# Graph kernel, first layer's dense turns: chunks taken alternately from a unit's halves, chunk tables streamed a turn at a time, a deeper ring of moving one-hots

## The chip, the cores and the metric

The kernel runs on one core of a Trainium2 chip. The metric is the device time of one execution in microseconds, as the median of several executions. TensorE appears as PE (weight loads as PEld), VectorE as DVE, ScalarE as ACT, GpSimd as POOL, SyncE as SP.

## The reference

6,250 nodes with 256 features, 200,000 edges sorted by destination, each with a weight. The part that this case is about is the first of two graph convolutions:

```
def _graph_conv(x, W, edge_src, edge_dst, edge_weight, n_nodes):
    support = x @ W
    msg = support[edge_src] * edge_weight[:, None]
    return jax.ops.segment_sum(msg, edge_dst, num_segments=n_nodes)
...
h = _graph_conv(features, W1, edge_src, edge_dst, edge_weight, n)
out = _graph_conv(h, W2, edge_src, edge_dst, edge_weight, n)
...
x = x + gnn(xn) + mix(xn)            # xn = layernorm(x); mix: linear attention
x = x + moe(layernorm(x))            # 16 experts, 2 a row
```

Both segment sums are done on unweighted features (the products with W1 and W2 are joined and come later), so that a layer is: for each destination node, the weighted sum of the rows of its sources.

## The kernel before

The edges lie in 1,584 chunks of 128. Each layer takes them in two ways at once. 768 chunks are **gathered**: GpSimd fetches the 128 source rows of a chunk by an indirect DMA (`gathers`, L606), and PE multiplies them with one-hots of the destination (`gathered`, L924). Four chunks make a step, 192 steps a layer, six steps a unit of 128 destinations. The other 810 chunks are **dense**: 27 units (turns) of 30 chunks. A dense turn has two stages.

*Build.* For each chunk PE multiplies a one-hot of the source's low 7 bits, times the weight (`lo_hot`, DVE, L1280, 128x128), with a moving one-hot of the pair of source tile and destination (`moving`, ACT, two activations L707 and L709, 128x343), into one of three PSUM banks (`build_chunk`, L899). DVE adds the 128x343 result into the slab, a 128 x 49 x 128 matrix in SBUF, at a destination offset that a register holds (`add_chunk`, L1295). Neighbouring chunks write overlapping columns, as the destinations are sorted, so an add waits for the add before it (`s_bev`). Rings: 10 `lohot`, 10 `mvs`, 3 banks; PE's chunk c waits for the add of chunk c-3.

*Apply.* When the last add is done, SP stores the slab's seven planes to DRAM (L477; the second layer loads them again), and PE multiplies the 49 slab tiles with the node features (`apply`, L911, seven tiles a plane). ACT clears each plane (`blanks`, L714) once it is applied and stored; the first add of the next turn waits for all seven (`s_z`). Meanwhile the first 10 `lo_hot` and `moving` of the next turn are made, two a plane.

The dense and gathered sums go through `take_dense` or `takes` (ACT copies, L732, L725), a placement matmul on PE (`place_dense` L943, `place_gathered` L934; their one-hots are `dense_hots` and `gathered_hots`, L1324) and an add by DVE into the layer's result (`place_add`, L1335). A turn also holds seven or eight gathered steps, at chunks 4, 11, 18, 25 and after planes 0, 2, 4 (and 5) (`SLOT1`), and DVE's destination one-hots for them (`half_hots`, L1317, L1319).

Every order is written out by hand; each engine runs its own list, held together by counting semaphores. The per-chunk numbers (`lo`, `nkey`, `off`) are computed once at the start by DVE and stay in SBUF (`l1tab`). In the second layer the slabs are only loaded and applied, then come the mix, the experts and the output.

## Time and profile before

| | |
|---|---|
| time, median of 3 | 3638.55 us (3625.0 to 3643.43) |
| the profiled execution | 3613.85 us, of which the profile's span is 3612.2 us |
| first layer's dense turns | from 78.4 us to about 1515 us of the span |
| PE busy over the span | 2916.3 us (81%) |
| DVE, ACT, POOL busy | 39%, 40%, 51% |
| mean granted TensorE clock | 0.927 of full speed |

The engines' busy shares are means over stages with different limits. In a line of the timeline stand the start and the length of a group of instructions, the engine, the line of the kernel, what it writes and reads, the count, and in brackets how long the engine was idle before and what it waited for.

### The profile page before, as it was taken

What the parts mean: (1) busy time and instruction counts of PE and PEld (TensorE: products, weight loads), DVE (VectorE), ACT (ScalarE), POOL (GpSimd) and SP (SyncE); (2) the same over time, 40 slices, a digit from 0 to 9 for tenths busy, and PEclk for the clock granted to TensorE, in tenths of its full rate; (3) what the DMA queues carried; (4) which work ended last, traced back from release to release, by engine and by line L of the source; (5) the groups of instructions that cost most, each with busy time, mean ns of one, the idle gap of its engine ahead of it and who ended that gap; (6) DMA issues with size and microseconds to landing.
All of it is one profiled execution on the core that took longest, in us unless ns stands there. A gap on an engine that the chain in (4) does not pass through costs nothing.

```text
span 3612.2 us, 49615 instructions
## 1 busy us (share of the span) xinstructions
PE 2916.3 (81%) x14732; PEld 2068.0 (57%) x14733; DVE 1420.1 (39%) x3945; ACT 1455.2 (40%) x3127; POOL 1844.7 (51%) x1924
## 2 busy tenths in 40 slices
PE   1799999899989999768988888888877648988930
PEld 0466556556656665546655666566546647777830
DVE  7544554554455446322222222222215541111157
ACT  4677776777777777300000000000004423333322
POOL 3555555545555555256666666666643651222235
PEclk9899999999999999979998999999988869999975
DMA  6344434434443443375555555555532334444454
GB/s 217 119 137 142 143 108 142 142 103 143 146 139 114 141 146 131 104 236 173 177 173 167 174 178 177 164 178 176 174 93 88 119 123 131 135 142 131 118 155 125
DMA packets 257759, 525.92 MB, mean 146 GB/s; under 512 B 47793, under 2 KB 144056, under 8 KB 257337
## 3 DMA queue, kind: packets, MB, share of 16 engines
q1 hardware_dynamic: 142492, 263.69, 22.4%
q0 software_dynamic: 84240, 228.40, 21.0%
q10 hardware_dynamic: 30832, 31.42, 2.7%
q8 instruction: 99, 1.62, 0.2%
q14 instruction: 96, 0.79, 0.1%
HBM read 387.33 MB, written 137.44 MB: 145 GB/s over the span
## 4 chain that ended last, share of the span: by engine, by line
PE 52%; issue 12%; DVE 11%; another core or an unknown queue 10%; ACT 6%; DMA 5%; SPq 3%; DVEq 1%; ACTq 1%; POOL 0%; POOLq 0%
PE bank L911 28%; PE bank L899 8%; PE sums L924 5%; DVE pa L1295 4%; DMA pa<-ys_d 4%; PE bank L1134 3%; PE bank L988 2%; PE bank L934 1%; ACT build L709 1%; ACT build L707 1%; PE sums L882 1%; ACT pa L833 1%; PE bank L943 1%; SPq L537 1%
## 5 line engine op out<-in xcount | busy, mean ns | idle before, releaser
L606 POOL DMA_INDIRECT pa<-xn_d,srcs x768 | 739.8, 963 | 667.4 <-PE sums L924 481.6
L606 POOL DMA_INDIRECT pa<-h_d,srcs x768 | 756.1, 985 | 398.2 <-issue 212.6
L911 PE MATMUL bank<-t1s,pa 128*128 128x256 f32 x2646 | 657.6, 398 | 100.0 <-issue 79.8
L899 PE MATMUL bank<-build 128*128 128x343 f32 x1620 | 559.9, 477 | 130.5 <-DVE build L1280 54.7
L1295 DVE TENSOR_TENSOR pa<-bank,pa 128x343 f32 x810 | 417.4, 515 | 603.8 <-ACT pa L714 462.8
L911 PE MATMUL bank<-t0s,pa 128*128 128x256 f32 x2646 | 612.5, 389 | 45.2 <-DVE pa L1295 37.4
L911 PEld LDWEIGHTS bank<-t1s,pa 128*128 128x128 f32 x2646 | 515.8, 199 | 231.5 <-issue 143.2
L911 PEld LDWEIGHTS bank<-t0s,pa 128*128 128x128 f32 x2646 | 504.7, 194 | 155.4 <-issue 86.2
L899 PEld LDWEIGHTS bank<-build 128*128 128x128 f32 x1620 | 279.8, 192 | 376.1 <-issue 298.1
L709 ACT ACTIVATE build<-build,ones 128x343 f32<-128x343 f32 x810 | 471.3, 582 | 26.3
L707 ACT ACTIVATE build<-build,l1tab 128x343 f32<-128x343 f32 x810 | 458.8, 566 | 37.3 <-issue 24.6
L665 POOL DMA_INDIRECT eo_d<-pa,eplc x109 | 107.3, 984 | 389.5 <-DVE pa L1614 348.2
L924 PE MATMUL sums<-pa,hots 128*32 128x256 f32 x3072 | 279.0, 399 | 33.5 <-issue 31.1
L714 ACT ACTIVATE pa<-zero 128x896 f32<-128x896 f32 x182 | 172.3, 947 | 330.2 <-PE bank L911 274.8
L1421 DVE TENSOR_REDUCE l1tab<-build 128x8 f32<-128x512 f32 x49 | 33.6, 686 | 592.6 <-ACT build L759 367.8
L1280 DVE TENSOR_SCALAR build<-iota_n,l1tab,wts 128x128 f32<-128x128 f32 x810 | 263.7, 353 | 0.0
L754 ACT ACTIVATE build<-bank 128x256 f32<-128x256 f32 x49 | 18.8, 384 | 502.0 <-remote 408.8
L1134 PE MATMUL bank<-build,pa 128*128 128x128 f32 x1744 | 218.0, 279 | 0.2 <-ACT build L845 0.2
L1134 PEld LDWEIGHTS bank<-build,pa 128*128 128x128 f32 x1744 | 208.1, 196 | 0.7 <-issue 0.6
L1122 PE MATMUL bank<-pa 128*128 128x256 f32 x872 | 207.6, 381 | 0.0
L1614 DVE TENSOR_TENSOR pa<-bank,pa 128x256 f32<-128x256 f32 x109 | 46.3, 425 | 389.2 <-PE bank L1122 389.2
L924 PEld LDWEIGHTS sums<-pa,hots 128*32 128x32 f32 x3072 | 69.1, 109 | 200.9 <-issue 199.4
(247 smaller groups left out, 2565.9 us busy)
## 6 DMA issues: line engine op xcount, KB each, us to landing
slab_d<-pa SPq DMA_DIRECT2D x189, 448.0 KB
pa<-slab_d SPq DMA_DIRECT2D x189, 448.0 KB
pa<-in_w ACTq DMA_DIRECT2D x32, 512.0 KB, 4.0
pa<-in_w SPq DMA_DIRECT2D x32, 512.0 KB, 3.7
pa<-ys_d SPq DMA_DIRECT2D x109, 130.0 KB
pa<-eo_d SPq DMA_DIRECT2D x49, 256.0 KB, 3.2
pa<-xn_d,srcs POOLq DMA_INDIRECT x768
pa<-h_d,srcs POOLq DMA_INDIRECT x768
```

The source lines that it names most:

```text
L606: pool.indirect_dma_start(gath[g % RING * QT + j], None, table, bass.IndirectOffsetOnAxis(ap=srcs[:, n:n + 1], axis=0)).then_inc(s_g[g % R ...
L665: pool.indirect_dma_start(eo_d, bass.IndirectOffsetOnAxis(ap=eplc[b][:], axis=0), eo[b], None, bounds_check=NONE - 1, oob_is_err=False).th ...
L707: act.activation(a, iotaw, ACT.Abs, bias=nkey[:, c:c + 1]).then_inc(s_mt, 1)
L709: act.activation(a, a, ACT.Relu, bias=ones[:, 0:1], scale=-1.0).then_inc(s_mv, 1)
L714: act.activation(plane(p), zero[:].broadcast_to([P, CT * P]), ACT.Copy).then_inc(s_z, 1)
L899: pe.matmul(bld[c % BLD][:, 0:WT], lohot[c % LR], mvs[c % MR], start=True, stop=True).then_inc(s_bmm, 1)
L911: ins = pe.matmul(app[:, 0:D], slab3[:, s, :], table[:, s * D:(s + 1) * D], start=s == 0, stop=s == T - 1)
L924: ins = pe.matmul(bank[u % 2][j * Q:(j + 1) * Q, 0:D], hoth[g // HK % HB][:, k % HK, j, :], gath[g % RING * QT + j], start=k == 0, stop=k ...
L1122: ins = pe.matmul(bank[4 + b][:, 0:D], hT[b][:, f, :], we2[b][:, f, :], start=f == 0, stop=f == 3)
L1134: ins = pe.matmul(bank[2 + b][:, f * P:(f + 1) * P], we1[b][:, a, f * P:(f + 1) * P], eyT[b][:, a, :], start=a == 0, stop=a == 1)
L1280: dve.tensor_scalar(lohot[c % LR], iota_n[:], lo[:, c:c + 1], wts[:, C0 + c:C0 + c + 1], ALU.is_equal, ALU.mult).then_inc(s_lo, 1)
L1295: dve.tensor_tensor(part, bld[c % BLD][:, 0:WT].rearrange("p (s w) -> p s w", w=W), part, ALU.add).then_inc(s_bev, 1)
```

## The change

Each unit's 30 chunks are now taken as 0, 15, 1, 16, ... (`chunk_at`), so that two adds in a row never touch the same columns of the slab, and an add waits only for the add before the last (except in the last turn). A flag at the start tests that such chunks lie at least seven destinations apart. The ring of moving one-hots grows from 10 to 18, of which 15 (three a plane) are made during the apply before; `lohot` from 10 to 12. SBUF for it comes from the tables: these go to DRAM at the start (`tab_d`, `off_d`), and SP loads 30 columns of them for each turn, two turns ahead, before it stores the slab. The dense unit's `place_add` and `dense_hots` move from the build (chunks 6 and 20) to the apply (planes 0 and 3).

```diff
-LR = 10
-MR = 10
+LR = 12
+MR = 18
+EARLY_LO = 12
+EARLY_MV = 15
+TABS = 2
...
-CREDIT = 12
+CREDIT = 20
 AHEAD = 4
-EARLY = 2
...
+        tab_d = dram("tab_d", [P, 2 * DC])
+        off_d = dram("off_d", [1, DC], I32)
...
-        l1tab = sb("l1tab", [P, 3 * DC])
+        tabs = [sb(f"tabs{b}", [P, 3, KB]) for b in range(TABS)]
+        offs = [sb(f"offs{b}", [1, KB], I32) for b in range(TABS)]
...
+        def chunk_at(m):
+
+            return m // 2 + m % 2 * (KB // 2)
...
+            sp.wait_ge(s_tab, 1)
+            sp.dma_start(tab_d, tab).then_inc(s_tst, 16)
+            sp.dma_start(off_d, off[0:1, :]).then_inc(s_tst, 16)
+            sp.wait_ge(s_tst, 32)
+
+            def turn_tables(i):
+                b = i % TABS
+                sp.wait_ge(s_lo, (i - TABS) * KB + KB)
+                sp.wait_ge(s_mv, (i - TABS) * KB + KB)
+                c = i * KB
+                sp.dma_start(tabs[b][:, 0:2, :], tab_d.rearrange("p (k c) -> p k c", k=2)[:, :, c:c + KB]).then_inc(s_tl[b], 16)
+                sp.dma_start(tabs[b][:, 2, :], wt_t[:, C0 + c:C0 + c + KB]).then_inc(s_tl[b], 16)
+                sp.dma_start(offs[b][:], off_d[:, c:c + KB]).then_inc(s_tl[b], 16)
+
             for i in range(NU):
                 sp.wait_ge(s_bev, i * KB + KB + BLD)
+                if i + TABS < NU:
+                    turn_tables(i + TABS)
                 for p in range(CT):
                     sp.dma_start(rows(slab_d, i)[:, p * CT * P:(p + 1) * CT * P], plane(p)).then_inc(s_slab[p], 16)
...
-            pool.memset(t1s[:, NCH + DC:T * D], 0.0).then_inc(s_t1z, 1)
+            pool.memset(t1s[:, SCRATCH:T * D], 0.0).then_inc(s_t1z, 1)
             pool.wait_ge(s_tab, 1)
-            pool.memset(t1s[:, 0:NCH + DC], 0.0).then_inc(s_t1z, 1)
+            pool.wait_ge(s_tst, 32)
+            pool.memset(t1s[:, 0:SCRATCH], 0.0).then_inc(s_t1z, 1)
             pool.wait_ge(s_xst, 16 * NC)
...
-            def moving(c):
-
+            def moving(i, m):
+
+                c = i * KB + m
                 a = mvs[c % MR]
+                if m == 0 and i >= TABS:
+                    act.wait_ge(s_tl[i % TABS], 48 * (i // TABS))
                 act.wait_ge(s_bmm, c - MR + 1 + CREDIT)
-                act.activation(a, iotaw, ACT.Abs, bias=nkey[:, c:c + 1]).then_inc(s_mt, 1)
+                k = chunk_at(m)
+                act.activation(a, iotaw, ACT.Abs, bias=tabs[i % TABS][:, 1, k:k + 1]).then_inc(s_mt, 1)
                 act.wait_ge(s_mt, c + 1)
                 act.activation(a, a, ACT.Relu, bias=ones[:, 0:1], scale=-1.0).then_inc(s_mv, 1)
...
-            for c in range(MR):
-                moving(c)
+            for m in range(EARLY_MV):
+                moving(0, m)
             for i in range(NU):
                 for m in range(KB):
-                    if m + MR < KB:
-                        moving(i * KB + m + MR)
+                    if m + EARLY_MV < KB:
+                        moving(i, m + EARLY_MV)
                     takes(steps_at(i, "m", m, 0), 0)
                 for p in range(CT):
                     if i < NU - 1:
-                        for m in range(p * EARLY, min(MR, (p + 1) * EARLY)):
-                            moving(i * KB + KB + m)
+                        for m in range(p * 3, min(EARLY_MV, (p + 1) * 3)):
+                            moving(i + 1, m)
                         blanks(i, p)
...
+            apart = exc.rearrange("p (k c) -> p k c", c=KB)[:, 0:NU - 1, 0:KB // 2 + 1]
+            off3 = off.rearrange("p (k c) -> p k c", c=KB)[:, 0:NU - 1, :]
+            link(dve.tensor_tensor(apart, off3[:, :, KB // 2 - 1:KB], off3[:, :, 0:KB // 2 + 1], ALU.subtract))
+            link(dve.tensor_reduce(reg[:, 4:5], apart, AX.XY, ALU.min))
+            link(dve.tensor_scalar(reg[:, 4:5], reg[:, 4:5], float(W), None, ALU.is_ge))
             link(dve.tensor_scalar(reg[:, 0:1], reg[:, 0:1], float(Q - 1), None, ALU.is_le))
+            link(dve.tensor_tensor(reg[:, 0:1], reg[:, 0:1], reg[:, 4:5], ALU.mult))
...
+            late_half = off.rearrange("p (k c) -> p k c", c=KB)[:, :, KB // 2:KB]
+            link(dve.tensor_scalar(reg[:, 5:6], reg[:, 3:4], float(P // 2), None, ALU.mult))
+            link(dve.tensor_scalar(off, off, reg[:, 1:2], None, ALU.mult))
+            link(dve.tensor_scalar(late_half, late_half, reg[:, 5:6], None, ALU.add))
...
+            for b in range(TABS):
+                link(dve.tensor_copy(tabs[b][:, 0:2, :], tab.rearrange("p (k c) -> p k c", k=2)[:, :, b * KB:(b + 1) * KB]))
+                link(dve.tensor_copy(offs[b][:], off[0:1, b * KB:(b + 1) * KB]))
...
-            def lo_hot(c):
-
+            def lo_hot(i, m):
+
+                c, k, a = i * KB + m, chunk_at(m), tabs[i % TABS]
                 dve.wait_ge(s_bmm, c - LR + 1 + CREDIT)
-                dve.tensor_scalar(lohot[c % LR], iota_n[:], lo[:, c:c + 1], wts[:, C0 + c:C0 + c + 1],
-                                  ALU.is_equal, ALU.mult).then_inc(s_lo, 1)
-
-            def offsets(c):
+                dve.tensor_scalar(lohot[c % LR], iota_n[:], a[:, 0, k:k + 1], a[:, 2, k:k + 1], ALU.is_equal, ALU.mult
+                                  ).then_inc(s_lo, 1)
+
+            def offsets(i):
+                if i >= TABS:
+                    dve.wait_ge(s_tl[i % TABS], 48 * (i // TABS))
                 return nc.values_load_multi_w_load_instructions(
-                    off[0:1, c:c + KB], engines=[mybir.EngineType.DVE], min_val=0, max_val=P - W,
+                    offs[i % TABS][0:1, :], engines=[mybir.EngineType.DVE], min_val=0, max_val=P - W,
                     skip_runtime_bounds_check_because="it is bounded by the subtraction from the span's end")[1]
 
-            def add_chunk(c, at):
-
-                if c % KB == 0:
-                    dve.wait_ge(s_z, c // KB * CT + CT)
+            def add_chunk(i, m, at):
+
+                c = i * KB + m
+                if m == 0:
+                    dve.wait_ge(s_z, i * CT + CT)
                 dve.wait_ge(s_bmm, c + 1 + CREDIT)
-                dve.wait_ge(s_bev, c + BLD)
-                part = slab3[:, :, bass.ds(at, W)]
+                dve.wait_ge(s_bev, c + BLD - (0 if i == NU - 1 else 1))
+                part = slab3[:, :, bass.ds(at[chunk_at(m)], W)]
...
-            for c in range(LR):
-                lo_hot(c)
+            for m in range(EARLY_LO):
+                lo_hot(0, m)
             dve.wait_ge(s_t1z, 2)
+            at = offsets(0)
             for i in range(NU):
-                at = offsets(i * KB)
                 for m in range(KB):
-                    c = i * KB + m
-                    add_chunk(c, at[m])
-                    if m + LR < KB:
-                        lo_hot(c + LR)
-                    if m == 6 and i > 0:
+                    add_chunk(i, m, at)
+                    if m + EARLY_LO < KB:
+                        lo_hot(i, m + EARLY_LO)
+                    all_gathered(steps_at(i, "m", m, 0), 0, t1s)
+                if i < NU - 1:
+                    at = None
+                    at = offsets(i + 1)
+                for p in range(CT):
+                    if p == 0 and i > 0:
                         place_add(1, GU + i - 1, t1s)
-                    if m == 20:
-                        dense_hots(i, 0)
-                    all_gathered(steps_at(i, "m", m, 0), 0, t1s)
-                for p in range(CT):
                     all_gathered(steps_at(i, "p", p, 0), 0, t1s)
                     if i < NU - 1:
-                        for m in range(p * EARLY, min(LR, (p + 1) * EARLY)):
-                            lo_hot(i * KB + KB + m)
+                        for m in range(p * 2, min(EARLY_LO, (p + 1) * 2)):
+                            lo_hot(i + 1, m)
+                    if p == 3:
+                        dense_hots(i, 0)
```

Not shown are moved scratch regions: the tables are computed in `t1s`, and the second layer's small weights, which lay in `l1tab`, now lie in `build`.

Three places in the instruction lists. First DVE, from the last add of a turn to the first add of the next one, before (L1295 is the slab add, L1280 `lo_hot`, L1317 and L1319 `half_hots`; TENSOR_LOAD fetches the 30 offsets):

```order
L1295 TENSOR_TENSOR pa<-bank,pa 128x49x7
L1317 TENSOR_TENSOR hots<-iota_n,drel 128x384
L1319 TENSOR_TENSOR hots<-hots,wts 128x384
L1280 TENSOR_SCALAR build<-iota_n,l1tab,wts 128x128 x10
L1284 TENSOR_LOAD l1tab
L1295 ISA
```

and after (L1349 is the slab add, L1331 `lo_hot`, L1371 and L1373 `half_hots`, L1389 `place_add`, L1378 `dense_hots`):

```order
L1349 TENSOR_TENSOR pa<-bank,pa 128x49x7
L1337 TENSOR_LOAD offs
L394 TENSOR_LOAD t_i
L394 ISA x2
L1389 ISA
L1389 TENSOR_TENSOR t1s<-bank,t1s 128x512
L1371 TENSOR_TENSOR hots<-iota_n,drel 128x384
L1373 TENSOR_TENSOR hots<-hots,wts 128x384
L1331 TENSOR_SCALAR build<-iota_n,tabs 128x128 x8
L1378 TENSOR_SCALAR hotp<-iota_n,drow 128x128 x2
L1331 TENSOR_SCALAR build<-iota_n,tabs 128x128 x4
```

The loads, the placement's add and its one-hots now stand in the apply stage, and 12 instead of 10 `lo_hot` do.

Second ACT, between the clearing of two planes in the apply stage, before (L714 clears a plane):

```order
L714 ACTIVATE pa<-zero 128x896
L707 ACTIVATE build<-build,l1tab 128x343
L709 ACTIVATE build<-build,ones 128x343
L707 ACTIVATE build<-build,l1tab 128x343
L709 ACTIVATE build<-build,ones 128x343
L714 ACTIVATE pa<-zero 128x896
```

and after (L751 clears a plane, L744 and L746 make a moving one-hot):

```order
L751 ACTIVATE pa<-zero 128x896
L744 ACTIVATE build<-build,tabs 128x343
L746 ACTIVATE build<-build,ones 128x343
L744 ACTIVATE build<-build,tabs 128x343
L746 ACTIVATE build<-build,ones 128x343
L744 ACTIVATE build<-build,tabs 128x343
L746 ACTIVATE build<-build,ones 128x343
L751 ACTIVATE pa<-zero 128x896
```

Three moving one-hots stand between two planes up to the fifth, where two stood.

Third SP's queue after the change, from the start's last stores through the first turn's slab stores; before, the slab stores (L477) followed directly on the stores of `xn_d`:

```order
L488 DMA xn_d<-t0s 128x7x256 x7
L491 DMA tab_d<-t1s 128x1620
L492 DMA off_d<-t1s 1x810
L500 DMA tabs<-tab_d 128x2x30
L501 DMA tabs<-in_wt_t 128x30
L502 DMA offs<-off_d 1x30
L509 DMA slab_d<-pa 128x896 x7
```

Two stores are new at the start, and three small loads stand ahead of the seven slab stores of each of the first 25 turns.

## Rows read from the trace of the kernel before

**Rows 1.** Busy time by stretch, one dense turn a row; first the first turn

```profile
core 0: us, PE busy (x) PEld busy (x) DVE busy (x) ACT busy (x) POOL busy (x), PEclk, DMA share, GB/s
78.42:150.91 72.49, 54.59 (x216) 32.66 (x216) 25.94 (x70) 44.58 (x80) 44.05 (x46) 0.81 0.41 130
...
412.18:463.22 51.04, 47.24 (x224) 31.11 (x223) 26.48 (x71) 38.58 (x70) 27.14 (x28) 1.00 0.41 136
...
515.39:573.92 58.53, 51.01 (x233) 32.62 (x231) 28.61 (x78) 38.58 (x70) 29.56 (x31) 0.94 0.37 122
...
1412.50:1462.42 49.92, 47.39 (x224) 31.04 (x223) 27.05 (x73) 38.59 (x70) 27.22 (x28) 1.00 0.42 139
```

**Rows 2.** Groups by line, 150 to 1500 us: PE's two large ones

```profile
L911 PE MATMUL bank<-t0s,pa 128*128 128x256 f32 x2500 | 579.4, 389 | 43.9 <-DVE pa L1295 36.2 <-issue 7.8
L899 PE MATMUL bank<-build 128*128 128x343 f32 x1560 | 530.5, 471 | 59.7 <-DVE pa L1295 35.4 <-issue 12.4 <-ACT build L709 11.8
```

**Rows 3.** Timeline of DVE in the build of the turn at 412.18

```profile
428.31 0.56 DVE L1317 TENSOR_TENSOR hots<-iota_n,drel 128x384 f32<-128x384 f32 x1
...
429.81 0.69 DVE L1335 TENSOR_TENSOR t1s<-bank,t1s 128x512 f32 x1 [0.35 <-issue]
430.42 0.50 DVE L1295 TENSOR_TENSOR pa<-bank,pa 128x343 f32 x1
430.84 0.34 DVE L1280 TENSOR_SCALAR build<-iota_n,l1tab,wts 128x128 f32<-128x128 f32 x1
431.12 0.52 DVE L1295 TENSOR_TENSOR pa<-bank,pa 128x343 f32 x1
...
437.04 0.52 DVE L1295 TENSOR_TENSOR pa<-bank,pa 128x343 f32 x1 [0.20 <-DVE pa L1295]
437.76 0.52 DVE L1295 TENSOR_TENSOR pa<-bank,pa 128x343 f32 x1 [0.20 <-issue]
```

**Rows 4.** Timeline of PE in the same turn: build's end, apply, next build

```profile
431.07 3.06 PE L899 MATMUL bank<-build 128*128 128x343 f32 x8 [1.82 <-DVE pa L1295]
...
434.63 2.58 PE L899 MATMUL bank<-build 128*128 128x343 f32 x8
438.42 3.26 PE L911 MATMUL bank<-t0s,pa 128*128 128x256 f32 x14 [1.21 <-DVE pa L1295]
441.61 0.64 PE L924 MATMUL sums<-pa,hots 128*32 128x256 f32 x8
...
461.95 1.90 PE L899 MATMUL bank<-build 128*128 128x343 f32 x6
```

**Rows 5.** Timeline of ACT in two apply stages

```profile
441.78 0.95 ACT L714 ACTIVATE pa<-zero 128x896 f32<-128x896 f32 x1 [5.57 <-DMA slab_d<-pa]
442.63 0.57 ACT L707 ACTIVATE build<-build,l1tab 128x343 f32<-128x343 f32 x1
...
443.72 0.56 ACT L707 ACTIVATE build<-build,l1tab 128x343 f32<-128x343 f32 x1
...
462.15 0.95 ACT L714 ACTIVATE pa<-zero 128x896 f32<-128x896 f32 x1 [2.07 <-PE bank L911]
...
712.20 0.95 ACT L714 ACTIVATE pa<-zero 128x896 f32<-128x896 f32 x1 [7.50 <-DMA slab_d<-pa]
```

**Rows 6.** Timeline of SP's queue, and hardware queues' share over 150 to 1500 us

```profile
707.17 6.94 SPq L477 DMA_DIRECT2D slab_d<-pa  x7
...
q1 hardware_dynamic: 26208, 83.50, 15.8%
```

**Rows 7.** Timeline of the start: issues on ACT's queue, DVE's tables, the first gather

```profile
2.94 0.68 ACTq L684 DMA_DIRECT2D build<-in_w1t  x1
...
48.54 1.00 DVE L1220 TENSOR_TENSOR l1tab<-pa,dk 128x810 int32<-128x810 f32 x1
...
73.41 2.09 POOL L597 MEMSET t1s<- 128x2394 f32 x1 [55.62 <-DVE scr L1157]
...
75.68 1.18 POOL L606 DMA_INDIRECT pa<-xn_d,srcs  x1 [0.17 <-issue]
```

More of the change, by code:

```diff
@@ L74 @@
 assert KV * KVT + 1 == T and KVT + 2 < NU
-assert KB % LR == 0 and KB % 5 == 0 and QK % HK == 0 and FG * P <= HB * HK * P
+assert KB % 2 == 0 and EARLY_LO <= LR and EARLY_MV <= MR and QK % HK == 0 and FG * P <= HB * HK * P
 class Links:
@@ L172, in gps_layer @@
         build = sb("build", [P, LR * P + MR * WT + WT])
-        l1tab = sb("l1tab", [P, 3 * DC])
+        tabs = [sb(f"tabs{b}", [P, 3, KB]) for b in range(TABS)]
+        offs = [sb(f"offs{b}", [1, KB], I32) for b in range(TABS)]
         srcs = sb("srcs", [P, C0], I32)
         dstf = sb("dstf", [P, C0])
-        wts = sb("wts", [P, NCH])
+        wts = sb("wts", [P, C0])
         mnmx = sb("mnmx", [MMP, MMC, 2], I32)
@@ L223, in gps_layer @@
         iotaw = build[:, LR * P + MR * WT:]
-        lo = l1tab[:, 0:DC]
-        nkey = l1tab[:, DC:2 * DC]
-        off = l1tab[:, 2 * DC:3 * DC].bitcast(I32)
+        SCRATCH = NCH + 4 * DC
+        tab = t1s[:, NCH + DC:NCH + 3 * DC]
+        lo, nkey = tab[:, 0:DC], tab[:, DC:2 * DC]
+        off = t1s[:, NCH + 3 * DC:SCRATCH].bitcast(I32)
         dgr = build[0:MMP, 0:MMC * P].bitcast(I32).rearrange("p (c e) -> p c e", e=P)
@@ L254, in gps_layer @@
         xT = build[:, 3584:3840].rearrange("p (a q) -> p a q", a=2)
-        r8 = l1tab[:, 1840:1856].rearrange("p (m h) -> p m h", m=2)
-        hsum = l1tab[:, 1856:1872]
+        after = build[:, 4024:5896]
+        r8 = after[:, 1840:1856].rearrange("p (m h) -> p m h", m=2)
+        hsum = after[:, 1856:1872]
         t1 = sq.rearrange("p (a n) -> p a n", a=2)
@@ L259, in gps_layer @@
         mixm = build[:, 0:512].rearrange("p (a n) -> p a n", a=2)
-        wq_s = l1tab[:, 0:512].rearrange("p (a n) -> p a n", a=2)
-        wo_s = l1tab[:, 512:1024].rearrange("p (a n) -> p a n", a=2)
-        bo_s, bet, gam = (l1tab[:, 1024 + k * D:1024 + (k + 1) * D] for k in range(3))
-        gw = l1tab[:, 1792:1824].rearrange("p (a n) -> p a n", a=2)
-        gb = l1tab[:, 1824:1840]
+        wq_s = after[:, 0:512].rearrange("p (a n) -> p a n", a=2)
+        wo_s = after[:, 512:1024].rearrange("p (a n) -> p a n", a=2)
+        bo_s, bet, gam = (after[:, 1024 + k * D:1024 + (k + 1) * D] for k in range(3))
+        gw = after[:, 1792:1824].rearrange("p (a n) -> p a n", a=2)
+        gb = after[:, 1824:1840]
         XR = 4
@@ L335, in gps_layer @@
         s_z = sem("s_z"); s_ap = sem("s_ap"); s_t1z = sem("s_t1z")
+        s_tst = sem("s_tst"); s_tl = [sem(f"s_tl{b}") for b in range(TABS)]
         s_obg = sem("s_obg"); s_hpg = sem("s_hpg"); s_plg = sem("s_plg"); s_pag = sem("s_pag")
@@ L403, in plane @@
             return slab[:, p * CT * P:(p + 1) * CT * P]
-        early = [(srcs[:], src_t[:, 0:C0]), (srcd, src_t[:, C0:C0 + DC]), (dsti, dst_t[:, 0:NCH]), (wts[:], wt_t[:, 0:NCH]),
+        early = [(srcs[:], src_t[:, 0:C0]), (srcd, src_t[:, C0:C0 + DC]), (dsti, dst_t[:, 0:NCH]), (wts[:], wt_t[:, 0:C0]),
+                 (tabs[0][:, 2, :], wt_t[:, C0:C0 + KB]), (tabs[1][:, 2, :], wt_t[:, C0 + KB:C0 + 2 * KB]),
                  (w1t_s, w1t.rearrange("(a p) n -> p a n", p=P)), (gw2_s, gw2.rearrange("(a p) n -> p a n", p=P))]
```

## Prediction

> **What bounds the kernel now.** I read the busy shares by dense turn first, then the groups by line in the first layer, then one turn on each engine in the timeline, then the start. The reader is to see four things.
>
> A dense turn takes 52.46 us: turn 1 begins at 150.91 and turn 26 at 1462.42, 25 turns later [rows 1]. PE is busy 47.2 to 51.0 us of one, so PE is what the turn is nearest to, and only its idle time can be won. Full clock and few waits give 49.92 us; the same work takes 51.04 us with more waits, and 58.53 us with waits and a granted clock of 0.94 [rows 1]. Between 150 and 1500 us PE is idle 43.9 us ahead of the apply and 59.7 us ahead of the build's products [rows 2]: 104 us, 3.9 a turn. Most of it is for DVE's slab add, 11.8 us for ACT.
>
> In the build DVE sets the pace. An add with a `lo_hot` behind it takes 0.70 us (430.42 to 431.12), and an add alone as much (437.04 to 437.76), although an add with a `lo_hot` lets the next instruction start after 0.42 us [rows 3]. The rest, 0.20 us idle and the add's tail, is the wait for the add before. PE needs 2.58 us for four chunks, 0.62 to 0.65 each [rows 4]. So in the last ten chunks PE could go on and doesn't; and a burst of `half_hots` and `place_add` (428.31 to 430.42, 2.1 us) shows as 1.82 us of PE idle at 431.07 [rows 3, 4].
>
> In the apply PE sets the pace: it starts at 438.42, 1.21 us after the last product, and the next build's first products start at 461.95 [rows 4]. ACT clears the last plane at 462.15 to 463.10, so the next turn's first add stands at 463.22, 24.94 us after the last add's end (437.76 plus 0.52) [rows 1, 3, 5]. The build between is 26.10 us in this turn (from 412.18), and 24.98 in the turn of 49.92.
>
> **The sum is made against the profiled execution,** 3613.85 us with a span of 3612.2; the median of the runs shown is 24.7 us above it, and I carry the difference in time over to the median.
>
> **Adds that wait for the last but one.** 12 adds a turn have no `lo_hot` behind them. The trace has no add behind an add without the wait. Its interval lies between 0.42 us (the start after an add, [rows 3]) and 0.72 (no gain); it is the same instruction, so I take 0.43. In this part PE then sets the pace, with 0.62.
>
> **Build after the change.** The first 18 adds carry a `lo_hot`: 17 intervals of 0.71 are 12.1 us. Bursts: four of seven gathered steps lie in the build, so 1.3 `half_hots` of 1.1 us and 0.7 `place_add` of 1.0 and 0.4 for its one-hots, 2.4 us in all, two thirds of them here: 1.6. So add 17 starts at 13.7. PE may be three banks ahead, so 9 products are left: 9 times 0.62, one gathered step of 0.57 (0.64 less the overlap, [rows 4]) and a third of a placement make 6.5; 0.6 for the product under way and 0.65 for the last add follow. Together 21.5 us; since PE and DVE don't always meet that well, I take 22.3. Against 26.1 and 25.0 that is 3.8 and 2.7 us, 3.2 in the mean. It contains the dense `place_add` and `dense_hots` (1.0 us of DVE), which go to the apply stage, where DVE waits some 20 us anyway; they would come back whole if DVE had work there. The gap of 1.21 us ahead of the apply should shrink to 0.8, as the last add no longer waits for its neighbour.
>
> **Fifteen early moving one-hots.** Twenty pairs of 1.09 us are 21.8 us of ACT in a build of 25; fifteen are 16.4, so ACT stays ahead of the shorter build (without them 21.8 would bound a build of 22.3). Their price is in the apply. ACT clears plane 0 at 3.4 to 5.0 us after the stage's start, when its store has landed (441.78 against 438.42; 712.20 against 707.17) [rows 4 to 6]. From there 12 pairs (13.1), six clearings at 0.86 and the last at 0.95 make 19.2 us. PE lets the last plane go so that clearing ends at 24.7 (463.10 less 438.42). So the store must land by 5.5, or the turn grows.
>
> **Three table loads ahead of the stores.** SP issues seven stores in 6.94 us [rows 6]. A load of 256 rows took 0.68 us to issue at the start [rows 7]; the three new ones have 256, 128 and 1 rows, so 1.0 to 2.0 us. Their 385 packets may cost nothing beside that, or as much as the large ones: 26,208 packets took 15.8% of 16 engines' 1350 us, 0.13 us each [rows 6], so 385 of them on 16 engines are 3.1 us. The store then lands at 4.4 to 10.1 us. The loads are small and nearest to the lower end; I take 5.8, which makes the turn 0.3 us longer. Per turn so far: 3.2 less 0.3, so 2.9 us.
>
> The page DMA: Bandwidth & Descriptors of the Trainium skill (Specifications) gives 512 bytes as the least transfer for the full rate, below which the engines do a read-modify-write; the table rows have 120 bytes. By that rule the landing would be at the upper end, which is the slower rival below; no row of the kernel before shows such a load.
>
> **Clock.** The mean turn is 2.0 us above the mean of the two full-clock turns (50.5). I expect a quarter to a third of this to go with PE's waits, 0.5 us. Together 3.4 us in each of 26 turns: 88 us.
>
> **The start.** DVE gets operations over 2047 columns more (1.00 us for 810, [rows 7]) and seven small ones, 3.5 us. The tables' store of 829 KB must land before POOL's memset, some 5 us (a plane of 448 KB lands in 3.4 to 5), and the memset covers 4824 columns where it took 2.09 us for 2394 [rows 7], 2.1 more. The first gather, at 75.68 now, moves by about 10 us. The first turn is 72.49 us at a clock of 0.81 [rows 1], with PE waiting for nothing the trace names, and might swallow this or add to it: 0 to 20, I take 11. **Sum:** 88 less 11 is 77 us: 3537 for a profiled execution like this one, 3562 for the median.
>
> **Rivals.**
> - *PE's records are all work (0.14).* I count PE's build at 22.5 us, but its records show more, which I read as waits inside them. If 47.3 us [rows 1] is work, a turn is 47.3 plus 0.8 and 0.5, and the 2.0 us of clock stay: 50.5. Gain 2.0 a turn, 52 less 11: 3598. For it: modelled ends. Against it: 0.62 us a chunk where PE runs freely.
> - *The clock stays full (0.14).* Turns fall to 50.5 less 2.9, 47.6 to 48.4: 106 to 126 us less 11, so about 3535. For it: the slowest turn has the lowest clock [rows 1]. Against: a turn with 1.82 us idle at once has 1.00. In the Trainium skill's page TensorE: Matmul & The Clock Gate (Part 1) the throttled state is the default and activity releases it; by this, fewer waits mean more turns at 2.4 GHz. The trace agrees as far as 0.94 stands beside 58.53 us.
> - *Stores too late: slower (0.07).* If the loads delay the landing to 10.1 us, plane 6 is cleared at 29.3, 4.6 us late each turn. Then 3.4 plus 0.3 less 4.6 is a loss of 0.9 a turn, 23 plus 11: 3673. It decides from a landing at about 8.7 us after the apply's start, where the 3 us net gain of a turn is eaten. For it: the loads stand first in the queue. Against it: only 385 packets.
> - *No change (0.08):* a landing at 8 to 9 us, or chunks that hardly gain because the bursts of DVE set the build: 3620 to 3655, about 3638. That the flag for distances fails is left out: 14 chunks are 1792 edges, some 56 destinations at 32 edges a node, against 7.
>
> **Numbers.** Forecast 0.57, at 3562, its own range 3540 to 3585. Faster by over 0.5% (about what a measurement here tells from no change) are the forecast and the first two rivals, 0.85; 0.08 and 0.07 for the others. The range reaches over most of the first two rivals: 3525 to 3605.
>
> **What the profile would show.** Adds at 0.43 to 0.62 us in the last twelve chunks; builds of 22 to 23 us, ACT waiting in them; PE's idle time ahead of L899 halved; plane 0 cleared at 5 to 6.5 us and the last at 24.7 to 25.5 after the apply's start; the first add of turn 1 some 5 to 10 us later than 150.91. I am wrong if the last plane is cleared later than 26, if the 12 adds stay at 0.7, or if the clock falls as often as before.

## The result and the profile after

The changed kernel takes 3585.17 us (median, 3580.34 to 3601.46) where the kernel before takes 3634.45, measured beside it: a ratio of 0.9873, 95% interval 0.983 to 0.9916, or 49 us less. The forecast was 77 us less. The profiled executions took 3613.85 us before and 3581.1 after, a difference of 33.

Time by stretch for the 25 turns from the first add of turn 1 to that of turn 26, the kernel before and the changed one (columns as in [rows 1]):

```profile
150.91:1462.42 1311.51, 1210.32 (x5588) 791.04 (x5587) 678.75 (x1813) 965.81 (x1730) 681.90 (x708) 0.98 0.40 133
```

```profile
156.91:1438.38 1281.47, 1198.06 (x5588) 794.66 (x5587) 665.08 (x1814) 958.08 (x1730) 691.96 (x708) 0.98 0.42 137
...
208.30:257.20 48.90, 46.71 (x224) 31.19 (x223) 27.74 (x76) 38.35 (x70) 27.50 (x28) 1.00 0.43 142
...
308.80:363.19 54.39, 49.74 (x222) 33.05 (x222) 25.73 (x71) 38.33 (x70) 27.75 (x28) 0.94 0.40 129
...
927.49:976.22 48.73, 46.76 (x224) 31.30 (x223) 26.81 (x73) 38.49 (x71) 26.68 (x28) 1.00 0.43 143
```

A turn takes 51.26 us in place of 52.46, so 25 turns win 30.0 us; the forecast was 3.4 a turn. Turn 1 begins 6.0 us later (156.91 against 150.91), and what lies behind the first add of turn 26 is 8.8 us shorter (2141.0 against 2149.8): 32.8 in all. Three turns of after stand above as single rows: two of 48.7 to 48.9 us, near the forecast (52.46 less 3.4), and one of 54.39.

By parts, read from the adds of each turn: the build takes 25.37 us in the mean (26.36 before, 22.3 forecast), and the part from the last add's end to the next turn's first 25.89 (26.10 before). The adds did what was forecast. DVE's timeline in the turn at 927.49:

```profile
935.49 0.51 DVE L1349 TENSOR_TENSOR pa<-bank,pa 128x343 f32 x1
935.91 0.34 DVE L1331 TENSOR_SCALAR build<-iota_n,tabs 128x128 f32<-128x128 f32 x1
936.16 0.51 DVE L1349 TENSOR_TENSOR pa<-bank,pa 128x343 f32 x1
...
946.83 0.17 DVE L1360 TENSOR_TENSOR drel<-dstf,dkr 128x24 f32<-128x24 f32 x1
...
948.54 0.69 DVE L1389 TENSOR_TENSOR t1s<-bank,t1s 128x512 f32 x1 [0.35 <-issue]
949.15 1.35 DVE L1349 TENSOR_TENSOR pa<-bank,pa 128x343 f32 x3
```

An add with a `lo_hot` takes 0.67 us (935.49 to 936.16; 0.70 in [rows 3]), and three adds in a row 1.35 us: less the 0.51 of the last one, they start 0.42 us apart, where [rows 3] have 0.72. Most adds of a build's last ten now start 0.58 us apart, as fast as PE makes products. PE's idle time by group, 150 to 1500 us, against [rows 2]:

```profile
L948 PE MATMUL bank<-t0s,pa 128*128 128x256 f32 x2575 | 590.1, 386 | 31.8 <-issue 17.9 <-DVE pa L1349 14.0
L936 PE MATMUL bank<-build 128*128 128x343 f32 x1560 | 524.3, 474 | 55.4 <-DVE pa L1349 27.2 <-issue 19.6 <-ACT build L746 7.6
```

What is put down to DVE went down (36.2 to 14.0 us ahead of the apply, 35.4 to 27.2 in the build), but "issue", time for which the profile names no releaser, went from 20.2 to 37.5 us. One such place, on PE, DVE and POOL, in the turn at 415.85:

```profile
424.94 3.16 PE L936 MATMUL bank<-build 128*128 128x343 f32 x10
430.11 2.62 PE L936 MATMUL bank<-build 128*128 128x343 f32 x4 [2.00 <-issue]
```

```profile
426.63 0.52 DVE L1349 TENSOR_TENSOR pa<-bank,pa 128x343 f32 x1
427.06 0.39 DVE L1331 TENSOR_SCALAR build<-iota_n,tabs 128x128 f32<-128x128 f32 x1
429.45 0.52 DVE L1349 TENSOR_TENSOR pa<-bank,pa 128x343 f32 x1 [2.00 <-PE bank L936]
```

```profile
419.36 0.95 POOL L639 DMA_INDIRECT pa<-xn_d,srcs  x1 [5.84 <-PE sums L961]
...
428.45 0.95 POOL L639 DMA_INDIRECT pa<-xn_d,srcs  x1 [0.30 <-issue]
434.01 0.95 POOL L639 DMA_INDIRECT pa<-xn_d,srcs  x1 [4.61 <-PE sums L961]
```

PE stands for 2.00 us with its one-hots ready. It is not PE that stops first, though. The add at 429.45 is that of the turn's 15th chunk, whose product PE had ended by 426.84 (the third of five in the group at 424.94, all of which are done by 428.10); adds that wait for their product start 0.13 us after it, this one 2.61. PE may be three banks ahead, so its 18th product waits for this add, and it starts at 430.11, 0.15 us after the add's end at 429.96. All 24 places in the 25 turns at which PE's "issue" of more than 0.06 us stands ahead of a product read the same: PE starts 0.15 us after an add's end. So the "issue" is a wait for DVE's add under another name. With it, PE's wait for adds went from 44.0 to 31.8 us ahead of the apply, and only from 47.8 to 46.8 in the build.

The add starts again at 429.45, where a series of eight gathers ends that POOL issued without a pause (419.36 to 429.40, 1.26 to 1.36 us each), while ACT makes its one-hots without a break (415.89 to 434.96). The same stretch of a turn before, on POOL:

```profile
415.69 0.95 POOL L606 DMA_INDIRECT pa<-xn_d,srcs  x1 [5.82 <-PE sums L924]
...
421.67 0.95 POOL L606 DMA_INDIRECT pa<-xn_d,srcs  x1 [1.25 <-PE sums L924]
...
427.72 0.95 POOL L606 DMA_INDIRECT pa<-xn_d,srcs  x1 [1.31 <-PE sums L924]
```

Before, POOL paused 1.25 us after each step of four gathers, since seven chunks of the build took 6.0 us (415.69 to 421.67) and four gathers 4.7. After, seven chunks take 5.0 (PE's gathered steps in this turn begin at 418.42 and 423.41), and the pauses close.

### The profile page after: what moved, and what is told of

Read it like the earlier page. It is cut to its first block, busy times and chain, and to the rows that moved or that the text cites. A ratio compares the mean times of both kernels' runs of the same rounds, so it can differ in the third digit from the quotient of the medians.

```text
span 3579.4 us, 49757 instructions
## 1 busy us (share of the span) xinstructions
PE 2900.7 (81%) x14732; PEld 2067.6 (58%) x14733; DVE 1416.0 (40%) x3956; ACT 1446.0 (40%) x3127; POOL 1848.0 (52%) x1924
## 4 chain that ended last, share of the span: by engine, by line
PE 60%; issue 11%; DVE 9%; DMA 5%; ACT 5%; another core or an unknown queue 5%; SPq 3%; ACTq 1%; POOL 0%; DVEq 0%; POOLq 0%
PE bank L948 30%; PE bank L936 11%; PE sums L961 6%; DMA pa<-ys_d 4%; PE bank L1171 3%; PE bank L1025 2%; PE bank L971 2%; DVE pa L1349 1%; ACT build L746 1%; ACT build L744 1%; PE sums L919 1%; PE bank L980 1%; PE bank L1159 1%; PE bank L1098 1%
## 5 line engine op out<-in xcount | busy, mean ns | idle before, releaser
L639 POOL DMA_INDIRECT pa<-xn_d,srcs x768 | 750.0, 977 | 627.8 <-PE sums L961 434.2
L948 PE MATMUL bank<-t1s,pa 128*128 128x256 f32 x2646 | 641.6, 391 | 77.1 <-issue 73.0
L936 PE MATMUL bank<-build 128*128 128x343 f32 x1620 | 552.5, 479 | 133.6 <-DVE build L1331 57.3
L1349 DVE TENSOR_TENSOR pa<-bank,pa 128x343 f32 x810 | 410.5, 512 | 554.1 <-ACT pa L751 400.8
L948 PEld LDWEIGHTS bank<-t1s,pa 128*128 128x128 f32 x2646 | 507.3, 196 | 203.8 <-issue 135.8
L936 PEld LDWEIGHTS bank<-build 128*128 128x128 f32 x1620 | 289.2, 194 | 363.0 <-issue 279.0
L746 ACT ACTIVATE build<-build,ones 128x343 f32<-128x343 f32 x810 | 471.2, 582 | 27.2 <-ACT build L744 0.9
L744 ACT ACTIVATE build<-build,tabs 128x343 f32<-128x343 f32 x810 | 458.8, 566 | 36.6 <-issue 28.4
L961 PE MATMUL sums<-pa,hots 128*32 128x256 f32 x3072 | 290.6, 400 | 56.1 <-issue 54.1
L751 ACT ACTIVATE pa<-zero 128x896 f32<-128x896 f32 x182 | 168.8, 937 | 286.6 <-DMA slab_d<-pa 187.2
L1477 DVE TENSOR_REDUCE build<-build 128x8 f32<-128x512 f32 x49 | 33.6, 686 | 605.2 <-ACT build L796 467.2
L1331 DVE TENSOR_SCALAR build<-iota_n,tabs 128x128 f32<-128x128 f32 x810 | 262.2, 359 | 1.9 <-issue 1.9
L1670 DVE TENSOR_TENSOR pa<-bank,pa 128x256 f32<-128x256 f32 x109 | 46.3, 425 | 383.4 <-PE bank L1159 383.4
```

The lines of the kernel that those rows point to most:

```text
L639: pool.indirect_dma_start(gath[g % RING * QT + j], None, table, bass.IndirectOffsetOnAxis(ap=srcs[:, n:n + 1], axis=0)).then_inc(s_g[g % R ...
L744: act.activation(a, iotaw, ACT.Abs, bias=tabs[i % TABS][:, 1, k:k + 1]).then_inc(s_mt, 1)
L746: act.activation(a, a, ACT.Relu, bias=ones[:, 0:1], scale=-1.0).then_inc(s_mv, 1)
L751: act.activation(plane(p), zero[:].broadcast_to([P, CT * P]), ACT.Copy).then_inc(s_z, 1)
L936: pe.matmul(bld[c % BLD][:, 0:WT], lohot[c % LR], mvs[c % MR], start=True, stop=True).then_inc(s_bmm, 1)
L948: ins = pe.matmul(app[:, 0:D], slab3[:, s, :], table[:, s * D:(s + 1) * D], start=s == 0, stop=s == T - 1)
```

## The experiments

Three theories went in. A: the gain comes from the adds' shorter interval, with ACT kept ahead; the loads cost nothing. B: the rings and the moved placements gained. G, formed after the first two groups of runs: what is missing went to stalls beside gathers that follow each other without a pause. Each run is compared with the kernel before on its own chip. The chips differ: on that of the first four runs the kernel before takes 3418 us, on those of the others 3613 to 3632. A row stands for each run where it is read: the 25 turns of the first layer, with the mean turn behind it in the text.

**order_alone.** The kernel before with `chunk_at` in `moving`, `lo_hot` and `add_chunk`, and

```diff
-                dve.wait_ge(s_bev, c + BLD)
+                dve.wait_ge(s_bev, c + BLD - (0 if c >= (NU - 1) * KB else 1))
```

> The kernel before with the order of the chunks and the looser wait alone (its flag does not test the distance of the halves). Theory A (the gain comes from adds that no longer wait for their neighbour, and needs ACT ahead): ten adds a turn have no one-hot behind them and go from 0.72 to 0.45 us, but ACT makes 20 pairs in the build (21.8 us) and the bursts of DVE stay, so the build falls from 26.4 to about 25.4 us, the start stays at 150.9 for turn 1, and the ratio is 0.992. Theory B (the longer rings and the moved placements are what gained): build 26.2 or more, ratio 0.998 to 1.002. Theory C (the order is all of it, the rest only costs): build 25.0 or less, ratio 0.984 or less.

Ratio 0.9879 (0.9862 to 0.9897), 41 us. Turn 50.08 us, build 24.5, turn 1 at 132.41. Theory B falls: the order and the wait alone win more than half of what any version won on this chip. Its result lies between A and C.

**full_wait.** The changed kernel with the strict wait:

```diff
-                dve.wait_ge(s_bev, c + BLD - (0 if i == NU - 1 else 1))
+                dve.wait_ge(s_bev, c + BLD)
```

> The changed kernel, in which each add waits for the one before again. Theory A: twelve adds go back from 0.45 to 0.72 us where PE would need 0.62; the build grows from 25.4 to 26.4 us, ratio 0.994. Theory B (rings and placements gained): build 25.4 to 25.7, ratio 0.987 to 0.989.

Ratio 0.9925 (0.99 to 0.9951); turn 50.35 us, build 24.65. The ratio is between the two theories. Set against tables_behind below, which differs from it by the loads' place as well, the build is 1.33 us longer where theory A had 1.0.

**early_ten.** `EARLY_MV = 10`, two a plane.

> The changed kernel with 10 moving one-hots in the apply (2 a plane) in place of 15 (3 a plane). Theory A: ACT has 20 pairs of 1.09 us in the build, is late for PE from about chunk 20, the build grows to 26.2 us with idle time of PE and DVE put down to ACT; ratio 0.993. Theory D (the build is set by DVE's bursts and PE's own stalls, ACT was never next): build 25.4 to 25.6, ratio 0.987 to 0.989.

Ratio 0.9841 (0.9823 to 0.9859); turn 49.30, build 23.74. PE's idle time ahead of the products, 150 to 1400 us:

```profile
L936 PE MATMUL bank<-build 128*128 128x343 f32 x1530 | 504.4, 467 | 32.9 <-DVE pa L1349 24.9 <-issue 6.9
```

Of the 32.9 us at most 1.1 are put down to ACT by name. But each of the 24 places of "issue" ends 0.10 us after ACT has made a moving one-hot, so up to 8.0 us are ACT's, 0.3 a turn. ACT is late, but theory A's size for it (a build of 26.2) falls.

**tables_behind.** In SP's loop the call of `turn_tables(i + TABS)` stands behind the seven stores.

> The changed kernel with a turn's three table loads issued behind its seven slab stores. Theory A: plane 0 is cleared 0.8 us earlier, at 4.1 us after the apply's start as in the kernel before, and the turn stays as it is since PE lets the last plane go later than that; ratio 0.986 to 0.988, apply part 25.9 us. The rival of late stores: the apply part falls by 0.5 us or more, ratio 0.983 or less.

Ratio 0.9801 (0.9784 to 0.9819). The rows of these four (full_wait, early_ten, tables_behind, order_alone), one fence for each:

```profile
137.78:1396.44 1258.66, 1192.90 (x5588) 784.49 (x5587) 680.15 (x1813) 957.83 (x1730) 690.10 (x714) 1.00 0.43 140
```

```profile
137.85:1370.33 1232.48, 1180.25 (x5588) 785.87 (x5587) 663.44 (x1813) 962.44 (x1730) 698.61 (x715) 1.00 0.44 143
```

```profile
137.00:1359.08 1222.08, 1174.81 (x5588) 790.08 (x5587) 664.15 (x1814) 959.19 (x1730) 699.26 (x715) 1.00 0.44 144
```

```profile
132.41:1384.41 1252.00, 1186.23 (x5588) 786.85 (x5587) 656.88 (x1814) 965.60 (x1730) 690.57 (x712) 1.00 0.42 140
```

With `tables_behind` plane 0 is cleared 3.6 us after the apply's start, early_ten (loads ahead) has 4.7, and the part from last add to first add is 25.57 us in both: the loads delay the clearing and cost the turn nothing. Against tables_behind (48.88 a turn) the strict wait costs 1.47 us, of which its build has 1.33, and the five moving one-hots 0.42. Builds on this chip repeat with a period of six turns, and of 27.9 us that PE is idle ahead of the build's products in tables_behind, 27.4 are for DVE: "issue" is all but gone. The changed kernel itself was not run there.

**after_again.** The changed kernel once more, with the kernel before on the same chip.

> The changed kernel itself, beside the kernel before on the chip of this call. The four runs before this one came from a chip on which the kernel before takes 3418 us in place of 3634, its first turn has a build of 25 to 29 us in place of 45, and the builds repeat with a period of six turns. Theory A (part of the missing gain was lost to stalls of PE that belong to the first chip): on such a chip the mean build is 23.3 to 23.6 us and the ratio 0.981 to 0.983. Theory E (the loss belongs to the kernel): the ratio is 0.987 again, and builds vary between 23 and 28 us.

Ratio 0.9937 (0.9913 to 0.9961): this chip is like that of the first pair, so theory A for the other kind was not tried; the builds vary from 23.5 to 28.5 us. Turn 52.50, build 26.16, first build 45.15 us. Two measurements of the same change, 0.9873 (0.983 to 0.9916) and 0.9937, thus have intervals that hardly touch, and in the profile its turns take as long as those of before.

**placements_back.** `place_add(1, ...)` behind chunk 6 and `dense_hots` behind chunk 20 again.

> The changed kernel with the dense placement's add and one-hots back in the build (behind chunks 6 and 20). Theory A: the add (1.0 us) lies in the part that DVE paces and the one-hots in the part that PE paces; the build grows by 0.7 us and the apply part stays; ratio 0.005 higher than the changed kernel on the same chip. Theory F: build within 0.3 us.

Ratio 0.9883 (0.985 to 0.9917), turn 51.59, build 25.62: not slower than the changed kernel on that chip but faster. The expectation falls.

**gathered_late.** The four gathered steps of the build behind the last twelve chunks:

```diff
-        SLOT1 = (("m", 4), ("m", 11), ("m", 18), ("m", 25), ("p", 0), ("p", 2), ("p", 4), ("p", 5))
+        SLOT1 = (("m", 19), ("m", 22), ("m", 25), ("m", 28), ("p", 0), ("p", 2), ("p", 4), ("p", 5))
```

> The changed kernel with its four gathered steps of the build behind chunks 19, 22, 25 and 28 in place of 4, 11, 18 and 25. Theory A (a burst of DVE for gathered steps in the first 18 chunks, where DVE sets the pace, costs its whole length; in the last 12 it hides behind PE): the build falls by 1.0 us against the changed kernel on the same chip, and nearly all builds take 22 to 23 us; ratio 0.007 lower. Theory F (PE's products and steps set the build): build within 0.3 us, same ratio.

Ratio 1.037 (1.0346 to 1.0394), the opposite of what was expected. DVE's and PE's timelines in the turn at 685.38:

```profile
709.93 0.69 DVE L1389 TENSOR_TENSOR t1s<-bank,t1s 128x512 f32 x1 [0.29 <-issue]
715.88 0.52 DVE L1349 TENSOR_TENSOR pa<-bank,pa 128x343 f32 x1 [5.26 <-remote]
```

```profile
706.72 0.84 PE L936 MATMUL bank<-build 128*128 128x343 f32 x2
716.54 3.32 PE L948 MATMUL bank<-t0s,pa 128*128 128x256 f32 x7 [8.98 <-DVE pa L1349]
```

PE has made its last product by 707.6. DVE's last add has its product and its plane, and stands 5.26 us for something that the profile can't name ("remote"). POOL had issued its gathers without a pause since 698.73, twelve of them by 713.8. In the 25 turns 82 adds stand for more than 0.5 us in this way, 204 us in all. This is what led to theory G.

**gathered_apply.** Two gathered steps in the build, five or six in the apply.

> The changed kernel with two gathered steps in the build (chunks 11 and 25) and five or six in the apply. Theory A: PE's own work only moves (0.57 us a step), but half of the bursts leave the part that DVE paces; the turn falls by 0.5 us, ratio 0.003 lower. Rival: six steps in 25 us outrun the gathers (about 1.25 us each, four a step), PE waits for them in the apply, and the turn grows by 1 us or more.

Ratio 1.0158 (1.0125 to 1.019). The build falls to 22.6 us, but the part behind it grows to 32.8. The turn does grow, as the rival said, but not by its mechanism: PE does not wait for gathers. ACT's clearings are late; 150 to 1400 us of the waits:

```profile
ACT pa L751 <- remote: 149.8, 40, 8.6
```

**gathers_small.** Rows of a gather of the first layer, behind the first five steps:

```diff
+                some = P if layer or s < RING else 16
-                    pool.indirect_dma_start(gath[g % RING * QT + j], None, table, bass.IndirectOffsetOnAxis(
-                        ap=srcs[:, n:n + 1], axis=0)).then_inc(s_g[g % RING], 16)
+                    pool.indirect_dma_start(gath[g % RING * QT + j][0:some, :], None, table, bass.IndirectOffsetOnAxis(
+                        ap=srcs[0:some, n:n + 1], axis=0)).then_inc(s_g[g % RING], 16)
```

> The changed kernel, in which each gather of the first layer behind the first five steps fetches 16 rows in place of 128 (the rest of the sums is left out; the number of instructions stays on every engine). Theory G (the stalls of PE and DVE, for which the trace names no releaser or another unit, come when gathers follow each other without a pause): on a chip where the kernel before takes about 3620 us they go, the mean build falls from 25.4 to 26.2 to about 23.4 us and the first build from 45 to 25 us; ratio 0.965 to 0.975. Theory H (the engines' own stream of instructions, whatever the gathers do): the build stays at 25 us or more and the first build at 45.

Ratio 0.9888 (0.9839 to 0.9937), turn 50.49, build 24.33; the first build stays at 45.8 us. Its row:

```profile
157.39:1419.63 1262.24, 1188.74 (x5588) 791.45 (x5587) 660.79 (x1813) 958.02 (x1730) 604.57 (x708) 0.99 0.21 75
```

With a gather shorter on POOL (604.57 us for 708, 0.85 each, in place of 0.98) the pauses come back: only two of 25 builds contain eight gathers in a row. Those two take 28.3 and 28.7 us, the other 23 on average 23.96. DMA's share is half (0.21), and those two builds are as long as any, so a stop doesn't need the full amount of data. But the stops don't go: 23 adds of these 25 turns stand for more than 0.5 us (24.9 us in all), and 19 of them in a series that has no fifth gather yet. Three parts of theory G's expectation failed: the first build did not change, the mean build is 24.33 us, not 23.4, and the ratio is 0.9888, not 0.965 to 0.975. This kernel leaves out 112 of a gather's 128 rows, and with them part of the sums.

**gathers_even.** The gathered steps spread over the turn, nothing else:

```diff
-        SLOT1 = (("m", 4), ("m", 11), ("m", 18), ("m", 25), ("p", 0), ("p", 2), ("p", 4), ("p", 5))
+        SLOT1 = (("m", 4), ("m", 13), ("m", 22), ("p", 0), ("p", 1), ("p", 3), ("p", 5), ("p", 6))
```

> The changed kernel with the gathered steps spread evenly in time: behind chunks 4, 13 and 22 and planes 0, 1, 3 and 5 (and 6 in a turn with eight), which is 7 us apart in place of 5.2 us in the build. Theory G: POOL pauses between steps, the stalls in the build go, build 23.5 us or less (one step less in it), apply part 0.6 us longer, turn 0.8 to 1.5 us shorter than the changed kernel's 51.3 to 52.5 on such a chip; ratio 0.975 to 0.982. Theory H: only PE's own work moves, turn within 0.3 us, ratio 0.987 to 0.994.

3532.91 us, ratio 0.977 (0.9738 to 0.9801), the fastest of all on such a chip. Turn 49.10, build 22.62, the part behind it 26.48. The 25 turns, POOL in one build and PE's groups:

```profile
157.25:1384.79 1227.54, 1180.78 (x5589) 784.36 (x5587) 665.07 (x1813) 958.34 (x1730) 690.58 (x709) 1.00 0.44 143
```

```profile
261.30 0.96 POOL L639 DMA_INDIRECT pa<-xn_d,srcs  x1 [2.82 <-PE sums L961]
...
267.64 0.95 POOL L639 DMA_INDIRECT pa<-xn_d,srcs  x1 [1.43 <-PE sums L961]
...
273.89 1.06 POOL L639 DMA_INDIRECT pa<-xn_d,srcs  x1 [1.43 <-PE sums L961]
```

```profile
L948 PE MATMUL bank<-t0s,pa 128*128 128x256 f32 x2573 | 587.9, 383 | 21.3 <-DVE pa L1349 20.5 <-issue 0.8
L936 PE MATMUL bank<-build 128*128 128x343 f32 x1560 | 509.5, 470 | 27.0 <-DVE pa L1349 22.8 <-issue 3.1 <-ACT build L746 0.6
```

POOL pauses 1.43 us between steps, and PE's "issue" falls from 37.5 to 3.9 us. The two longest builds left, 26.3 and 28.0 us, are those in which a series of eight gathers had begun 4.5 and 4.8 us before the build. The build also has three gathered steps in place of four, and the even spread was not run on the chip of the first four runs, so what the spread gives where nothing stops is not known.

**tables_behind_2.** tables_behind on this chip.

> The kernel of the run tables_behind once more, on this call's chip. Theory A: against the changed kernel it gains nothing, since the clearing of plane 0 decides no turn: ratio 0.987 to 0.994 on a chip where the kernel before takes about 3620 us, 0.980 on one where it takes about 3420. Rival (the loads ahead of the stores delay something that counts): 0.983 or less on a chip of the first kind.

Ratio 0.9933 (0.9911 to 0.9955), turn 51.81, build 25.89: nothing gained, as with after_again.

**before_even.** The kernel before with the even `SLOT1`.

> The kernel before with the gathered steps spread as in the run gathers_even, and nothing else. Theory G (it was the shorter build of the change that closed the pauses between the gathers, so the kernel before has little to win by the spread): the four builds of 28.2 to 29.7 us among its 25 fall to 26.5 or less, the mean build falls by 0.5 to 1.0 us, the apply part grows by 0.6 us, the turn stays within 0.5 us of 52.5; ratio 0.995 to 1.000. Rival (the spread is a gain by itself, whatever the order of the chunks, and the change keeps its 49 us beside it): the turn falls by 1.3 us or more; ratio 0.99 or less.

3580.51 us, ratio 0.9855 (0.9827 to 0.9884). Its row:

```profile
149.59:1438.27 1288.68, 1204.72 (x5588) 775.39 (x5587) 678.09 (x1813) 967.20 (x1730) 680.25 (x709) 1.00 0.41 135
```

The turn falls by 0.91 us to 51.55, between what the two theories said, and the ratio is the rival's. The build falls by 1.2 us, the part behind it grows by 0.3. So the spread is worth something by itself. In these profiles it takes 0.9 us from a turn of before and 2.2 to 3.4 from one of after (51.26 and 52.50): under the even spread the change wins 2.45 us a turn, 61 us in 25, where it won 30.0 in the first pair of profiles (these profiles were taken at different times and not all on one chip, and the same kernel's 25 turns took 1281 and 1312 us in two of them, so the second figure is the less certain). The medians don't show this difference: 0.977 over 0.9855 is 0.991, so the change wins some 0.9%, or 31 us, under the even spread, and 0.9873 and 0.9937 stand for it without. That the spread helps the changed kernel more than the kernel before thus rests on the profiles alone and is not shown by the times.

**The count that ties them together.** In each trace, for the builds of turns 1 to 25: in how many a series of eight or more gathers (no pause of POOL over 0.6 us) begins in the first 20 us and has its eighth gather before the last add's end; and how many slab adds start more than 0.5 us after both their product and DVE's instruction before were done (of 725, a turn's first left out), with the sum of this time:

| kernel | such builds, mean us | the others, mean us | adds that stand | their sum, us |
|---|---|---|---|---|
| before | 5, 28.7 | 20, 25.8 | 16 | 16.2 |
| after | 16, 26.2 | 9, 23.9 | 45 | 46.3 |
| after_again | 23, 26.3 | 2, 24.1 | 60 | 68.0 |
| placements_back | 13, 26.8 | 12, 24.3 | 34 | 33.4 |
| tables_behind_2 | 16, 26.9 | 9, 24.1 | 49 | 55.4 |
| gathers_small | 2, 28.5 | 23, 24.0 | 23 | 24.9 |
| gathers_even | 0 | 25, 22.6 | 4 | 8.2 |
| before_even | 0 | 25, 25.2 | 5 | 7.4 |
| tables_behind | 21, 23.1 | 4, 24.5 | 0 | 0 |

In the changed kernel 145 of the 725 adds start beside the fifth or a later gather of a series, and 42 of the 45 that stand are among them. None of the 449 `lo_hot` in these builds starts more than 0.5 us after the instruction before it, and every idle time of PE over 0.5 us ends within 0.3 us of an add's end. So it is the adds that stand, and PE behind them.

On the chip of the first four runs it does not hold (the table's last row): there tables_behind issues 16 gathers in a row and no add stands:

```profile
239.29 0.96 POOL L639 DMA_INDIRECT pa<-xn_d,srcs  x1 [5.84 <-PE sums L961]
...
258.62 0.96 POOL L639 DMA_INDIRECT pa<-xn_d,srcs  x1 [0.30 <-issue]
261.65 0.95 POOL L639 DMA_INDIRECT pa<-xn_d,srcs  x1 [2.08 <-PE sums L961]
```

## Why the prediction was right in its direction and too high in its size

- **Adds that wait for the last but one: right.** 0.42 us where 0.43 was taken, and PE's 0.58 a chunk where 0.62 was. Full_wait against tables_behind prices the whole of it at 1.47 us a turn.
- **Build after the change: the step that failed.** It gave 22.3 us and a gain of 3.2; 25.37 were measured, a gain of 0.99. PE's idle time ahead of the products, which was to be halved, went from 59.7 to 55.4 us. Two things were missing.
  - The sum had no term for what a shorter build does to POOL. By it the pauses between the gathered steps close, and eight gathers follow each other in 16 of 25 builds instead of 5. These builds are 2.3 us longer than the others (26.2 against 23.9), since slab adds in them stand with their product ready. The weighted loss is 1.5 us a turn; before it was 0.6, so 0.9 of the missing 2.2 us lies here. That the build falls to 22.62 us and the standing adds from 46.3 to 8.2 us with the steps spread is shown; that the closed pause is the cause is argued from this and from the count, and the 19 adds that stand in gathers_small without a fifth gather speak against it as the only cause.
  - A build without such a series takes 23.9 us, not 22.3; before it took 25.8, so its gain is 1.9 us in place of 3.2. The working took bursts behind chunk 18 as hidden. The one at chunk 25 isn't: it holds DVE from 946.83 to 949.15, longer than PE's banks last, as PE's timeline there shows:

```profile
946.77 2.00 PE L936 MATMUL bank<-build 128*128 128x343 f32 x6
949.80 0.82 PE L936 MATMUL bank<-build 128*128 128x343 f32 x2 [1.03 <-DVE pa L1349]
951.41 1.75 PE L948 MATMUL bank<-t0s,pa 128*128 128x256 f32 x7 [0.80 <-DVE pa L1349]
```

- **The gap ahead of the apply: right**, 0.80 us in 16 of 25 turns; where a turn's last adds stand it is up to 2.85, and 1.22 in the mean.
- **Placements out of the build: wrong in what they are worth.** They were to save DVE 1.0 us, most of it on the path. Put back, they cost nothing measurable (51.59 us a turn against 52.50), perhaps since the slower build also has fewer builds with eight gathers in a row, 13 against 23, and 33.4 us of standing adds against 68.0.
- **Fifteen early moving one-hots: right in the direction.** ACT holds PE up for 7.6 us in all from 150 to 1500 us (11.8 before); without five of them the turn is 0.42 us longer, of which ACT's lateness is up to 0.3. A bound of 21.8 us and a build of 23.7 hardly touch.
- **Three table loads ahead of the stores: right, a little too dear.** Plane 0 is cleared 4.92 us after the apply's start in the mean (4.13 before; 5.8 forecast). The turn pays nothing where 0.3 was taken. The rule of 512 bytes cited from the Trainium skill (DMA: Bandwidth & Descriptors, Specifications) would have brought the landing near the upper end, 10.1 us; loads with rows of 120 bytes moved it by 0.8, so no run here shows such a price.
- **Clock: wrong.** 0.5 us a turn were to come back. Nine of 25 turns have a granted clock below 1.00 after, eight before. With most of the stops gone (gathers_even) two have, and in after_again, with the most, 18. This was one of the prediction's own signs of being wrong. Of the others, the last plane is cleared at 25.6 us in the mean, later than 26 in six turns, and the adds came down from 0.7.
- **The start: half.** POOL's first gather is at 83.88 instead of 75.68, 8.2 us later where 10 were taken, and the first turn takes 70.33 us, not 72.49, so that 6.0 remain of 11.
- **The sum.** 88 less 11 was forecast, over 26 turns, and 30.0 less 6.0 measured, over 25, with 8.8 more behind turn 26, where the change does nothing that I can name; in before_even that stretch is 2140.6 us too, so it differs by as much between two profiles. Where no add stands, on the other chip, tables_behind wins 69 us of 3418.
- **The rivals.** That PE's records are all work (50.5 us a turn) is refuted by the turns of 48.7 to 48.9. That the clock stays full came nearly true only without most of the stops. Stores too late: the last plane's clearing ends 0.98 us after PE has let the plane go in nearly every turn of either kernel, refuted. No change (3620 to 3655) is refuted by 3585. What did come was not on the list: the gathers' rhythm.

**Open:** why the adds stand, and why not on every chip. In turns 1 to 25 it is the adds on DVE, and PE behind them. In the first build of after, DVE, ACT and POOL all begin again within 0.2 us of each other:

```profile
117.76 0.58 ACT L744 ACTIVATE build<-build,tabs 128x343 f32<-128x343 f32 x1 [6.61 <-remote]
```

```profile
117.86 0.52 DVE L1349 TENSOR_TENSOR pa<-bank,pa 128x343 f32 x1 [7.03 <-remote]
```

```profile
117.95 0.95 POOL L639 DMA_INDIRECT pa<-xn_d,srcs  x1 [3.96 <-remote]
```

That first build took 44.8 to 48.0 us in every run on such chips, small gathers or not (gathered_apply is left out, which has other steps there), and 25 to 29 us on the other. Whether the engines lack instructions or their semaphores are late isn't settled by these runs; that no `lo_hot` ever stands, while adds do, speaks for the adds' own waits.

## What to carry to other kernels

Before you shorten a stage, look at what else is paced by it: here a queue of gathers was let on by every seventh chunk, and its pauses of 1.3 us were the first thing that the shorter stage used up. An edit that spaces such work evenly over the turn cost one line and brought as much as the whole change. Measure a gain of one per cent on more than one chip: the same two kernels gave 0.9873 and 0.9937, and adds stand for 46.3 us in one trace and for 68.0 in the other. And where a profile names no releaser, look at what ended just before the engine started again: here PE's "issue" ended 0.15 us after an add in the changed kernel, and 0.10 us after a one-hot of ACT's in early_ten.
